# Short bf16 products of all-ones ahead of units 20 to 26 of the adjacency sums

## What is computed

```
h = layernorm(x)
for W, b in three levels:
    m = concat([h[dst], h[src] - h[dst]]) @ W + b      # per edge
    h = relu(segment_sum(m, dst) / max(count(dst), 1))
x = x + concat([all four h]) @ Wf + bf
x = x + sum over the best 2 experts of gelu(layernorm(x) @ W1[e] + b1[e]) @ W2[e] + b2[e]
```

## Time and profile before

| | us |
|---|---|
| median of 3 runs (lowest, highest) | 185.26 (185.14, 185.63) |
| the profiled execution | 185.45 |
| its span, first to last instruction | 183.5 |
| PE, PEld busy | 150.9, 127.2 |
| DVE, ACT, POOL busy | 95.9, 66.8, 70.8 |

### The profile page before, as it was taken

One profiled execution on the slowest core, in us unless ns is written; L12 is line 12 of the kernel. 1 busy time (PEld: TensorE's weight loads), 2 busy tenths in 40 slices (PEclk: granted clock), 3 DMA queues, 4 the chain that ended last, 5 costly groups with the idle time before them and its releaser, 6 DMA issues.

```text
span 183.5 us, 3109 instructions
## 1 busy us (share of the span) xinstructions
PE 150.9 (82%) x1005; PEld 127.2 (69%) x1006; DVE 95.9 (52%) x243; ACT 66.8 (36%) x187; POOL 70.8 (39%) x96
## 2 busy tenths in 40 slices
PE   0362474999998999999998899969999999999710
PEld 0341262998898999899998789826777776666600
DVE  6799999768799640322149779330332232222200
ACT  8234776457312231231120751132434334333300
POOL 8503940000498068120003000062566665563662
PEclk9999999999999999999999999999999999999985
DMA  4639999940000500200001689310333443432332
GB/s 144 184 31 374 365 367 369 363 163 4 5 4 0 172 9 0 63 4 0 0 4 54 197 242 397 138 57 29 61 57 60 67 73 63 85 57 29 57 57 29
DMA packets 16055, 20.33 MB, mean 111 GB/s; under 512 B 1754, under 2 KB 12388, under 8 KB 15908
## 3 DMA queue, kind: packets, MB, share of 16 engines
q1 hardware_dynamic: 12692, 15.75, 26.4%
q0 software_dynamic: 2544, 3.54, 11.5%
q10 hardware_dynamic: 800, 0.79, 1.2%
HBM read 16.81 MB, written 3.26 MB: 109 GB/s over the span
## 4 chain that ended last, share of the span: by engine, by line
PE 58%; DVE 18%; POOL 9%; DMA 5%; issue 5%; ACT 2%; POOLq 1%; ACTq 0%; DVEq 0%
PE cnt_ps L1637 10%; PE bank L1618 6%; PE g_ps L1618 5%; PE bank L1499 4%; PE cnt_ps L1341 3%; DVE hot_lo L960 3%; POOL w_lo L574 3%; PE cnt_ps L1499 3%; PE cnt_ps L1631 2%; DVE a_hi L1038 2%; DMA out_rows<-y_sb,row_put 2%; DMA out_rows<-y_sb,row_of 2%; PE g_ps L1334 2%; PE g_ps L1336 2%; PE g_ps L1335 2%
## 5 line engine op out<-in xcount | busy, mean ns | idle before, releaser
L1637 PE MATMUL cnt_ps<-w_sb,h_t 128*128 x104 | 24.8, 381 | 2.2 <-ACT h_t L869 2.2
L1637 PEld LDWEIGHTS cnt_ps<-w_sb,h_t 128*128 128x128 f32 x104 | 18.8, 190 | 4.6 <-issue 2.6
L629 POOL DMA_INDIRECT out_rows<-y_sb,row_of x10 | 15.9, 1591 | 15.2 <-DMA out_rows<-y_sb,row_of 9.9
L623 POOL DMA_INDIRECT xg<-x_rows,row_of x12 | 12.0, 1003 | 22.4 <-DMA x_rows<-x_f 19.0
L1390 PE MATMUL bank<-hot_key,hot_lo 125*128 125x45 bf16 (+4 forms) x80 | 8.3, 243 | 10.9 <-DVE hot_key L963 6.8
L1276 DVE TENSOR_TENSOR y_sb<-cnt_ps,b_bc 128x256 f32<-128x256 f32 x13 | 5.5, 425 | 20.1 <-PE cnt_ps L1637 20.1
L960 DVE TENSOR_TENSOR hot_lo<-iota_lo,edge_rel 125x1024 bf16<-125x1024 int16 x20 | 13.9, 697 | 2.0 <-PE g_ps L1390 2.0
L1390 PEld LDWEIGHTS bank<-hot_key,hot_lo 125*128 125x128 bf16 x80 | 5.3, 123 | 13.2 <-DVE hot_key L963 12.2
L1618 PE MATMUL bank<-w_sb,xt 128*128 x28 | 13.4, 600 | 0.1
L1341 PE MATMUL cnt_ps<-ident 128*128 128x128 f32 x100 | 12.0, 277 | 0.0
L1272 DVE TENSOR_TENSOR h_pre<-bank,b_bc 128x512 f32<-128x512 f32 x7 | 4.8, 691 | 13.1 <-PE bank L1618 13.1
(11 more groups left out here) (289 smaller groups left out, 420.6 us busy)
## 6 DMA issues: line engine op xcount, KB each, us to landing
w_sb<-in_L_ffn_W SPq DMA_DIRECT2D x16, 512.0 KB, 10.2
b_bc<-in_L_ffn_b SPq DMA_DIRECT2D x8, 256.0 KB, 5.5
w_stage<-in_L_gnn_W SPq DMA_DIRECT2D x3, 512.0 KB, 6.0
w_stage<-in_L_gnn_Wf SPq DMA_DIRECT2D x4, 256.0 KB, 7.3
b_bc<-in_L_ffn_b SPq DMA_DIRECT2D x1, 1024.0 KB, 12.5
x_rows<-x_f ACTq DMA_DIRECT2D x1, 640.0 KB, 8.8
x_sb<-in_x SPq DMA_DIRECT2D x1, 512.0 KB
out_rows<-x_sb SPq DMA_DIRECT2D x1, 512.0 KB
```

The lines of the kernel that those rows point to most:

```text
L623: pool.indirect_dma_start(out=xg[:, b, :], out_offset=None, in_=x2_rows, in_offset=bass.IndirectOffsetOnAxis(ap=rows, axis=0)).then_inc(x_ ...
L629: pool.indirect_dma_start(out=out, out_offset=bass.IndirectOffsetOnAxis(ap=rows, axis=0), in_=y_sb[:, b, :], in_offset=None, compute_op=AL ...
L1637: last = pe.matmul(bank[3][:, 0:D], h_t[:, k, :], w2_sb[:, ds(e, 1), k, :], start=k == 0, stop=k == HC - 1)
```

## The change

A helper `keep_clock(k, n)` waits for the pane of chunk k to be free and then issues n bf16 products of ones_bf (128 x 128) by itself, 128 columns each, into that pane. It stands ahead of the pairs 20/21, 22/23 and 24/25 with n = 6 and ahead of the pair 26/27 with n = 32: 50 products and their 50 weight loads. Their results are not read: the first product of the chunk that follows in the pane starts a new sum. The wait of `keep_clock` is that of the chunk behind it; the wait for hot_made comes only after the added products. The wait on `consts` makes sure that ones_bf is written.

```diff
-WARM_DEGREE, WARM_NORM, WARM_GATE, WARM_ROUTE, WARM_GATHER = 10, 12, 4, 10, 24
+WARM_PAIR, WARM_H0, WARM_NORM, WARM_GATE, WARM_ROUTE, WARM_GATHER = 6, 32, 12, 4, 10, 24
...
-            for u in range(20, 28, 2):
+            def keep_clock(k, n):
+
+                pe.wait_ge(a_written, k - PANES + 1)
+                for _ in range(n):
+                    pe.matmul((bank[0], bank[1], g_ps[1], g_ps[2])[k % PANES][:, 0:P], ones_bf[:], ones_bf[:],
+                              start=True, stop=True, skip_group_check=True)
+
+            pe.wait_ge(consts, 6)
+            for u in range(20, 26, 2):
+                keep_clock(chunks_before(u), WARM_PAIR)
                 sum_pair(u)
+            keep_clock(chunks_before(26), WARM_H0)
+            sum_pair(26)
             pe.wait_ge(w_split, 1)
             pe.wait_ge(ht_ready, 4)
             ys_product(0, 0)
```

## The result

The changed kernel takes 191.23 us (median of 4 runs, 190.92 to 193.04) against 185.44 (185.14 to 185.97, 4 runs) for the kernel before beside it: a ratio of 1.0296, 95% interval 1.0232 to 1.036. It is slower, far outside the range that was predicted. The profiled execution took 191.21 us with a span of 189.2 (before: 185.45 and 183.5).

The account below looks back on a forecast made before the run. DVE was taken to bound the stretch to 31.98 us, then TensorE to 38.5. The 32 ending at 33.03 plus 3.98 put unit 30 at 37.01 against 37.69, so 185.26 - 0.68 = 184.6 us, range 184.0 to 186.2.

Parts of the forecast that it names:

- What bounds the kernel: Up to 31.98 us the path is DVE's, entered through units 20 and 21; from there to 38.5 us it is TensorE's.
- The price of one product: One added 128-column product on TensorE costs 0.107 us at the low clock level and 0.057 us at the high level.
- Six ahead of pair 20/21: Nothing hides these six: 0.64 us on DVE's path, hot_key of units 26 and 27 ready at 32.56 instead of 31.92.
- The 32: Ahead of pair 26/27 on TensorE: run from 31.2, take 1.83 us at the high level and end at 33.03.
- early rise: TensorE's clock rises by about 31.4 us, before the 32 begin: unit 30 0.68 us sooner, 184.6 us; chance 0.42.
- the doubt about its moment: The clock's rise on TensorE might come later; each of the 32 run at the low level costs 0.05 us more.
- What it gives back: TensorE from unit 26 to unit 30 takes 3.98 us at the high level instead of 5.71, 1.73 less.
- The step that failed: Behind unit 30, DVE, POOL and PE move along as a chain, so the 0.68 us gain reaches the end unshortened.
- the sign: TensorE idle at 59.64 us by more than the earlier 0.56 us would show an unmoved wait and overturn the forecast.
- Late rise: Clock rises near 33.8 us, 24 of the 32 run low: 0.52 us slower, 185.8; chance 0.22 including a dearer product.
- no rise: The products don't raise TensorE's clock, all 32 run low to 34.62: 1.54 us slower, 186.8 us; chance 0.06.

Follow-up runs that it names:

- h_inplace: Changed kernel with the 32 products alone, no sixes, never-taken loop cut from 8 units to 2, 40 never-executed products behind it: 186.28 us, ratio 1.0002.
- b_less43: Kernel before with TensorE's never-taken loop cut from 8 units to 2 and 50 never-executed products behind it: 186.03 us, ratio 1.0009.
- p_inplace: Changed kernel with the three sixes alone, no 32, never-taken loop cut from 8 units to 2, 53 never-executed products behind it: 187.18 us, ratio 1.0073.
- a_late_load: Changed kernel with SyncE's weight load for level 2 held back until TensorE's first product of level 1 is finished: 191.34 us, ratio 1.0285.
- w_less60: Changed kernel with 14 wide products instead of 50, never-taken loop cut from 8 units to 2, 27 never-executed products behind it: 184.91 us, ratio 0.9941.
- a_less43: Changed kernel with all its 50 products, only TensorE's never-taken loop cut from 8 units to 2, nothing put behind it: 184.42 us, ratio 0.994.
- w_less30: Changed kernel with 14 wide products instead of 50, never-taken loop cut from 8 units to 2, 42 never-executed products behind it: 184.87 us, ratio 0.999.
- b_dead50: Kernel before with 50 products added in TensorE's branch that this input never takes: 193.83 us, ratio 1.0435.
- a_dead78: Changed kernel with 78 products added in TensorE's never-taken branch, moving later code by one whole block of 256 instructions: 186.85 us, ratio 1.0044.
- a_wide: Changed kernel with the same 6400 columns of ones in 14 products of 384 and 512 columns instead of 50: 185.48 us, ratio 0.997.

## Why the prediction was wrong

*What bounds the kernel* held: DVE's path up to unit 26, TensorE's from there to unit 30, and the two clock levels read from spacings.

*The price of one product* held. 32 in 30.95 to 32.75 are 1.80 us, 0.056 each, against the 0.057 taken. The 81 ns that the Trainium skill gives for such a stream (page "TensorE: Matmul & The Clock Gate", section "Back-to-back issue gap") would have been 2.59 us; they aren't seen here.

*Six ahead of pair 20/21* held: 27.02 to 27.66 is the 0.64 us, and the next hot_lo on DVE starts at 28.47 (28.46 predicted, 27.82 before); hot_key of units 26 and 27 ends at 32.57 (32.56).

*The 32* began at 30.95 instead of 31.2 and let unit 26 go at 32.75 instead of 33.03. The clock was up for all of them. So the case "early rise" was the one that came, and the doubt about its moment, on which more than half of the chance was spent, was not where the risk lay.

*What it gives back:* 32.75 to 36.58 is 3.83 us, against 3.98 taken and 5.71 before. Unit 30 came 1.11 us sooner, not 0.68; the sum was 0.28 us too careful at the start and 0.15 in the stretch.

What the two kinds are for was not predicted. The clock had risen before the 32, and without any six: in `h_inplace`, which has none, about 13 of the 32 ran at the high level, up to the fall at 31.0 (worked out from their 2.77 us, with 0.056 and 0.107 us to a product). In `b_less43`, which has no added product, the view shows the fall at the same 31.0, when TensorE had stood still since 30.0. So this fall isn't made by the gap of 1.99 us, which ended only at 32.0, nor was it prevented by filling the gap. With the sixes it doesn't come: `p_inplace` keeps the clock up through its gap and loses it at 34.5, 1.9 us behind the gap's end. With both kinds no fall shows. The prediction had a clock that must be raised; what was to be done was to keep it from falling, and each kind does away with one fall. (The view shows these falls only in some profiles; in before it stays at 1.00 where the spacings are those of the low level.) What brings on the fall at 31.0 stays open.

*The step that failed* is the last of the sum: "So the 0.68 goes to the end unshortened; I see no wait behind it on anything that doesn't move along." One thing didn't move along, the program's place. The prediction costed what the 50 products do when they run, and nothing of what their 101 instructions (with a wait) do by lying ahead of the branches of the degrees and the three levels. Against the 1.1 us gained stand 0.7 and 3.0 us of waiting for code, then 1.5 of low clock behind the longer wait. The prediction did name the sign, TensorE idle at level 1's first product by more than 0.56 us: it was 3.47, but as an open door, with no rival, no price and no chance.

No rival came in its place either. "Late rise" and "no rise" end on the slower side, by the wrong mechanism: in the profile of the changed kernel the clock is high where they have it low.

*What stays open.* When exactly a packet starts (level 2 of `a_late_load`). The 0.7 us behind the last product, in the output's scatters: a 13th packet starts at 176.0 us, near them, but no run takes it away alone. The second low stretch (near 112 us after, +1.1 us): a low stretch between 104 and 115 us turns up in some profiles of both kinds and not in others (`w_less60` and `b_less43` have it, `a_less43` not), so it is not put down to the change.

## What to carry to other kernels

An instruction costs also by where it stands: in a program with branches, an addition ahead of them, executed or not, can make a branch wait for its code, so look in the profile for TensorE idle "issue" at and shortly behind branches and for the moments of the instruction packets, and set every taken branch and its target against the blocks of 256 instructions. Count in the compiled program: the count that the expectations went by was off by 35 instructions, and within that much the wait at level 2 goes from none (7 earlier) to 1.2 us (27 later). Judge a small change only beside a control that has its later code in the same place, and check in the control's profile that it has no wait of its own, and where it matters give the branches a good place (here by shortening a half that is never taken, which alone turned 1.03 into 0.994). And an expected gain that crosses a branch to reach the end deserves a rival that says what the branch costs.

## What the runs showed of the hardware

- A wait for TensorE's code ends 2.1 to 2.9 us behind the start of the packet (for example 75.59 to 77.86 in before, 74.47 to 76.61 in `w_less30`, 48.91 to 51.28 in `b_dead50`, 58.76 to 61.25 in `a_late_load`, 81.5 to 84.39 in `b_dead50`), and 3.5 us behind it with 0.79 MB of weights in flight (58.73 to 62.23 after). Where the engine had something else to do meanwhile, only a part shows: in before 0.21 us.
- The waits stand at edges 256 instructions apart, to the instruction: code moved by 4 instructions waits 4 instructions sooner in its half (before and `w_less30`), code moved by 256 at the same one (`a_dead78`).
- 50 products that are never executed: 193.83 us against 185.7 or so. 78 of them on top of the change: 186.85 against 191.23.
- The wait costs again by the clock: after 3.47 us of idle time 0.50 was granted from about 63.1 to 66.5 us, and 1.5 us more were lost. In all three profiles with an idle time of 2.5 to 3.5 us at level 1 (after, `b_dead50`, `a_late_load`) the clock fell and the work from there to the gathered sums took 12.3 to 12.7 us; in the other thirteen it took 11.0 to 11.2.
- A wait for code may carry the name of a releaser that was done long ago: 1.53 us "<-DVE ut_lo" ahead of level 2 in `a_wide`, 1.99 "<-DVE a_hi" in `b_dead50`.
- 32 products bf16 of 128 columns with a weight load each ran at 0.056 us apiece at 2.4 GHz.
